# Mixture-of-experts kernel on one core: 39 routed units in each layer instead of 40

## The chip, the core and the metric

The kernel runs on one core of a Trainium2 chip. The metric is the device time of one execution in microseconds. TensorE (PE in the rows) multiplies matrices, VectorE (DVE) and ScalarE (ACT) work elementwise, GpSimd (POOL) and SyncE (SP) mostly issue DMAs here. Every engine runs its own instruction stream in order, and the streams meet only through semaphores that one raises and another waits for.

## The reference

4096 tokens of width 128 pass through four residual blocks: an angular attention, a mixture of experts, a linear attention, and the same mixture of experts again. The mixture is what the change touches, and it is computed twice, once in each "layer":

```
logits = xf @ gate_w + gate_b
top_w, top_i = jax.lax.top_k(logits, K)            # K = 2 of E = 8 experts
gw = jax.nn.softmax(top_w, axis=-1)
combine = (gw[:, :, None] * jax.nn.one_hot(top_i, E)).sum(axis=1)
for e in range(E):
    h = gelu(xf @ w1[e] + b1[e])                   # 128 -> 512
    out = out + combine[:, e:e+1] * (h @ w2[e] + b2[e])   # 512 -> 128
shared = gelu(xf @ ws1 + bs1) @ ws2 + bs2
```

## The kernel before

**Routing by units.** The kernel computes an expert only for the tokens that chose it. GpSimd scatters each token's row twice, once for each chosen expert, into a DRAM buffer `routed_rows` with one region for each expert. A region is then worked on in units of RU = 256 rows. An expert's last unit is usually not full, so the count of units depends on the routing. With 8192 rows in all and at most 255 missing in each of eight regions, no routing needs more than (8192 + 8 * 255) // 256 = 39 units. The count in the code is fixed: `UNITS` rounds 39 up to 40. A table that VectorE makes (`table`, L1669 to L1701) gives each unit its first row (`URI`) and its expert's place in the weights (`UW`) and the biases (`UB`). Units beyond the need are pointed at spare regions behind the eight; their rows are padding whose destinations lie in a spare part of the result buffer. They are computed and stored like any other unit. Which units are needed is known only at run time, but unit 39, the 40th, never is.

**The pads.** `pad_rows` holds PADS = E + SPARE blocks of 256 padding rows, made once by GpSimd. SyncE stores one block at the end of each region in each layer (L467), and one in each of the SPARE = 8 spare regions in layer 0 (L472), before it loads the first unit.

**The routed stage.** `steps` (L61) writes a software pipeline: step s runs each part of the stage for unit s minus that part's lag. With RING = 6 buffers there are some straight steps, then a loop over six steps, then straight steps to the end. For unit u:

- SyncE, `load_rows` (L479 to L490): two DMAs, rows and tail, into ring slot u % 6, once unit u - 6 has left it.
- TensorE, lag 0, `routed_up`: 12 matmuls of 128x256 (L1161 to L1163), into one of three places in PSUM.
- ScalarE, `routed_gelu` (L899): four activations of 128x256.
- VectorE, lag 1, `routed_dest` (L1744) and `routed_split` (L1752, L1755): the hidden values as a high and a low half-precision part.
- TensorE, lag 3, `routed_down`: 24 matmuls of 128x128 (L1177 to L1179); it waits for the split of its unit and for `routed_out` of the unit two before, which frees its PSUM bank.
- VectorE, lag 3, `routed_out` (L1764): scales the result by the gate weight. In a step it comes behind the split of the unit two later.
- GpSimd, `store_results` (L662): two indirect DMAs of 128 rows each, which scatter the results to the tokens' places in `expert_results`.

When the scatters of all units of a layer have landed, SyncE loads `expert_results` back in eight pieces (L499) and VectorE adds them to X (L1432, L1434). In layer 0 the linear attention follows from there, in layer 1 the output.

The functions of both versions, as far as the diff touches them:

Of the kernel before, what the change touches and what calls it, by code (L numbers as in the profile page):

```python
# [16 lines left out]
ALU = mybir.AluOpType  # L17
ACT = mybir.ActivationFunctionType
F32 = mybir.dt.float32
F16 = mybir.dt.float16  # L20
BF16 = mybir.dt.bfloat16
U32 = mybir.dt.uint32
I32 = mybir.dt.int32
# [3 lines left out]
P = 128  # L27
LN_EPS = 1e-5
HEADS, HEAD_DIM = 16, 8
E = 8  # L30
# [4 lines left out]
ROW = 2 * P + 4  # L35
# [6 lines left out]
RS_TILES = 2  # L42
# [5 lines left out]
def wait(engine, semaphore, value):  # L48

    if isinstance(value, int) and value <= 0:  # L50
        return
    engine.wait_ge(semaphore, value)
# [77 lines left out]
def build(nc, x_in, ln_w, ln_b, k_w, q_w, a_bias, w_qkv, w_out, gate_w, gate_b,  # L130
# [5 lines left out]
    assert D == P and S == GT  # L136
    REGION = TOK + RU
    UNITS = (2 * TOK + E * (RU - 1)) // RU
    UNITS = -(-UNITS // 4) * 4
    SPARE = UNITS - 2 * TOK // RU  # L140
    HT = NT // 2
    PADS = E + SPARE
# [10 lines left out]
    with ctx:  # L153
        def sb(name, shape, dt=F32):
            return ctx.enter_context(nc.sbuf_tensor(name, shape, dt))
# [11 lines left out]
        def carve(shape):  # L167

            n = int(np.prod(shape))
            ap = big[:, carved[0]:carved[0] + n]  # L170
            carved[0] += n
            names = "abcd"[:len(shape)]
            sizes = dict(zip(names, shape))
            return ap.rearrange(f"p ({' '.join(names)}) -> p {' '.join(names)}", **sizes)
# [21 lines left out]
        iota_e, region_of = sb("iota_e", [P, 1, E]), sb("region_of", [P, E])  # L196
        down_e = sb("down_e", [P, 1, E])
        chain_on = sb("chain_on", [P, E, NT // 2])
        unit_no = sb("unit_no", [P, UNITS])
        iota_i = sb("iota_i", [P, UNITS], I32)  # L200
        dest = sb("dest", [P, NT, 2], I32)
        halfneg, halfpi, tiny = sb("halfneg", [P, 1]), sb("halfpi", [P, 1]), sb("tiny", [P, 1])
        amax, amaxr = sb("amax", [P, 4]), sb("amaxr", [P, 4])
# [24 lines left out]
        XHL = carve([4 * TPG * ROW]).bitcast(F16).rearrange("p (r t c n) -> p r t c n", r=4, t=TPG, c=2)  # L228
        HF = SC

        pad_rows = carve([PADS * RS_TILES * ROW // 2]).bitcast(F16).rearrange("p (e r n) -> p e r n",
                                                                              e=PADS, r=RS_TILES)
        parts_at = carved[0]
        XNG = carve([2, TPG, D])
        carved[0] = parts_at
# [14 lines left out]
        CN, CNI, NTI = sb("CN", [P, E]), sb("CNI", [P, E], I32), sb("NTI", [P, E], I32)  # L250
        PADF, PADI = sb("PADF", [P, E]), sb("PADI", [P, E], I32)
        NTF, CUM, JUMP = sb("NTF", [P, E]), sb("CUM", [P, E]), sb("JUMP", [P, E])
        UE, UR, UM = sb("UE", [P, UNITS]), sb("UR", [P, UNITS]), sb("UM", [P, E, UNITS])
        URI = sb("URI", [P, UNITS], I32)
        UW, UB = sb("UW", [P, UNITS], I32), sb("UB", [P, UNITS], I32)
        routing_at = carved[0]
        LG, MX = carve([NT, E]), carve([NT, 2])
        OH, CB2, EX, PLACE = carve([2, HT, E]), carve([2, HT, E]), carve([E, HT]), carve([HT, E])
# [6 lines left out]
                                                                                   r=RS_TILES)  # L265
# [79 lines left out]
        def turns(layer, k):  # L345

            return layer * (-(-(UNITS - k) // RING))
# [71 lines left out]
        def table_values(engine_type, table, stride):  # L419

            def values(u, n):
                _, found = nc.values_load_multi_w_load_instructions(
                    table[0:1, bass.ds(u, n)], [engine_type], min_val=0, max_val=(E - 1) * stride,
                    skip_runtime_bounds_check_because="the table's experts are clamped")
                return found
            return values
# [5 lines left out]
        def _(sp):  # L432
# [28 lines left out]
            for layer in range(2):  # L461
# [17 lines left out]
                def load_rows(u, h, k):  # L479

                    wait(sp, s["rh_ready"], layer * UNITS + u - RING + 1)
                    wait(sp, s["dst_ready"], layer * UNITS + u - RING + 1)
                    row = sp.value_load(URI[0:1, bass.ds(u, 1)], min_val=0,
                                        max_val=E * REGION + (SPARE - 1) * RU)
# [29 lines left out]
        def _(pool):  # L514
            made = [0]

            def const(ins):
                made[0] += 1
                ins.then_inc(s["consts_made"], 1)
                pool.wait_ge(s["consts_made"], made[0])  # L520
# [6 lines left out]
                                     base=0, pattern=[[-1, P]], channel_multiplier=1))  # L527
# [5 lines left out]
                                     base=0, pattern=[[1, P]], channel_multiplier=-1))  # L533
# [3 lines left out]
            for view, inner in ((heads, [[0, HEAD_DIM]]), (mask[:, D:D + HEADS], [])):  # L537
                const(pool.affine_select(out=view, in_=view, compare_op=ALU.is_ge, fill=0.0, base=0,
                                         pattern=[[-HEAD_DIM, HEADS]] + inner, channel_multiplier=1))
                const(pool.affine_select(out=view, in_=view, compare_op=ALU.is_ge, fill=0.0,  # L540
                                         base=HEAD_DIM - 1, pattern=[[HEAD_DIM, HEADS]] + inner,
                                         channel_multiplier=-1))
# [3 lines left out]
            const(pool.tensor_scalar(down_e[:, 0, :], iota_e[:, 0, :], -1.0, float(E), ALU.mult, ALU.add))  # L546
            const(pool.memset(chain_on[:], 1.0))
            const(pool.memset(chain_on[:, :, 0:1], 0.0))
            const(pool.iota(iota_i[:], pattern=[[1, UNITS]], base=0, channel_multiplier=0))
            const(pool.tensor_copy(unit_no[:], iota_i[:]))  # L550
            const(pool.iota(dest[:], pattern=[[2 * GT, NG], [2, TPG], [1, 2]], base=0,
                            channel_multiplier=2 * TPG))
# [4 lines left out]
                                     pattern=[[-(E + 1), len(TERMS)]], channel_multiplier=1))  # L557
            const(pool.affine_select(out=term_of[:], in_=term_of[:], compare_op=ALU.is_ge, fill=0.0, base=E,
                                     pattern=[[E + 1, len(TERMS)]], channel_multiplier=-1))
# [34 lines left out]
            def x_scale(n, h, k):  # L594
                if k % 2 == 0:
# [19 lines left out]
                      pattern=[[RU, PADS], [P, RS_TILES], [0, 1]], base=2 * TOK,  # L615
                      channel_multiplier=1).then_inc(s["pads_made"], 1)
# [571 lines left out]
        def _(dve):  # L1188
# [235 lines left out]
            for layer in range(2):  # L1424
# [244 lines left out]
                def table():  # L1669
                    n = [layer * TABLE_STEPS]  # L1670

                    def step(ins):
                        n[0] += 1
                        ins.then_inc(s["table_step"], 1)
                        dve.wait_ge(s["table_step"], n[0])

                    one = slice(0, 1)
                    step(dve.tensor_tensor(CN[one], PADF[one], region_of[one], ALU.subtract))
                    step(dve.tensor_scalar(CNI[one], CN[one], float(RU - 1), None, ALU.add))

                    if layer:
                        dve.wait_ge(s["pads_stored"], 16 * (E * layer + SPARE))
                        for k in range(RING):
                            dve.wait_ge(result_stored[k], 16 * RS_TILES * turns(layer, k))
                    step(dve.tensor_copy(PADI[one], PADF[one]))
                    step(dve.tensor_scalar(NTI[one], CNI[one], RU.bit_length() - 1, None, ALU.logical_shift_right))
                    step(dve.tensor_copy(NTF[one], NTI[one]))
                    step(dve.tensor_tensor_scan(CUM[one], onesf[one, 0:E], NTF[one], 0.0, ALU.mult, ALU.add))
                    step(dve.tensor_scalar(JUMP[one], NTF[one], float(-RU), float(REGION), ALU.mult, ALU.add))
                    begun, by_unit = UM[one], UM[one].rearrange("p e u -> p u e")  # L1690
                    step(dve.tensor_tensor(begun, unit_no[one].unsqueeze(1).to_broadcast([1, E, UNITS]),
                                           CUM[one].unsqueeze(2).to_broadcast([1, E, UNITS]), ALU.is_ge))
                    step(dve.tensor_reduce(UE[one], by_unit, AX.X, ALU.add))
                    step(dve.tensor_tensor(begun, begun, JUMP[one].unsqueeze(2).to_broadcast([1, E, UNITS]),
                                           ALU.mult))
                    step(dve.tensor_reduce(UR[one], by_unit, AX.X, ALU.add))
                    step(dve.scalar_tensor_tensor(UR[one], unit_no[one], float(RU), UR[one], ALU.mult, ALU.add))
                    step(dve.tensor_scalar(UW[one], UE[one], float(E - 1), float(HB * P), ALU.min, ALU.mult))
                    step(dve.tensor_scalar(UB[one], UE[one], float(E - 1), float(HB), ALU.min, ALU.mult))
                    assert n[0] == (layer + 1) * TABLE_STEPS  # L1700
                    dve.tensor_copy(URI[one], UR[one]).then_inc(s["table_ready"], 1)  # L1701

# [12 lines left out]
                def later_table(n, h, k):  # L1715

                    if isinstance(n, int) and n == 7:
                        table()
# [80 lines left out]
```

## Time and profile before

| | us |
|---|---|
| median of three runs | 866.07 |
| lowest, highest | 865.18, 870.05 |
| the profiled execution's own time | 864.79 |
| its span, first to last instruction | 863.0 |

The page of the profile gives TensorE 568.6 us of matmul work (66% of the span), VectorE 579.4 us (67%), ScalarE 403.1 us (47%) and GpSimd 416.4 us (48%). The routed stage of layer 0 lies between about 307 and 465 us of the span, that of layer 1 between about 683 and 842 us. An instruction's row shows its start, its duration, and, in brackets, how long its engine was idle before it and what ended that wait. "Remote" stands for a wait whose end the profile can't put down to an engine.

### The profile page before, as it was taken

Reading aid. Unit: us, or ns where it says so; the run is one execution under the profiler, and the core shown is the slowest. Engines: PE = TensorE matmul, PEld = TensorE weight load, DVE = VectorE, ACT = ScalarE, POOL = GpSimd, SP = SyncE. Lnnn points to the kernel's source line nnn. Section 1 sums busy time; section 2 is a strip of 40 time slices with the busy share of each in tenths; the row PEclk is TensorE's granted clock in tenths of the full one; section 3 lists DMA queues with packets and bytes.
Section 4 is the critical chain, followed back from the end, with each engine's and each line's share of the span. In section 5 each row is a group of like instructions: output and inputs, shape, how many; then the busy total and the mean of one; then the engine's idle time right before and its main releaser. Section 6 shows DMA issues by size and latency. Waiting matters only on the chain.

```text
span 863.0 us, 17109 instructions
## 1 busy us (share of the span) xinstructions
PE 568.6 (66%) x5073; PEld 415.5 (48%) x5074; DVE 579.4 (67%) x1215; ACT 403.1 (47%) x744; POOL 416.4 (48%) x377
## 2 busy tenths in 40 slices
PE   1565726624587788888881678643658998889850
PEld 0222326523354467677671566431235776667740
DVE  5899677977768357676673588856138586676644
ACT  1363899725423155555450577553023374445520
POOL 3097102141788716666664122367734045665670
PEclk9977968965588889999996899766559998999975
DMA  9200000000112523433314100011102233333218
GB/s 290 68 0 0 1 0 1 0 0 10 47 44 78 112 48 79 82 71 74 78 48 150 49 25 2 16 35 50 50 25 74 40 67 66 75 77 69 64 40 295
DMA packets 90829, 51.83 MB, mean 60 GB/s; under 512 B 71482, under 2 KB 79892, under 8 KB 90772
## 3 DMA queue, kind: packets, MB, share of 16 engines
q1 hardware_dynamic: 81556, 32.07, 15.4%
q0 software_dynamic: 9216, 19.02, 7.1%
q8 instruction: 32, 0.52, 0.3%
q14 instruction: 25, 0.20, 0.1%
HBM read 16.28 MB, written 24.30 MB: 47 GB/s over the span
## 4 chain that ended last, share of the span: by engine, by line
PE 38%; DVE 25%; issue 15%; ACT 10%; another core or an unknown queue 5%; DMA 3%; POOL 3%; DVEq 0%; SPq 0%; ACTq 0%; POOLq 0%
PE PC L1177 6%; PE PC L1179 5%; PE PC L1178 4%; PE PA L1161 2%; PE PA L1162 2%; PE PA L1163 2%; DVE PB L1248 2%; PE PA L943 2%; PE PC L1140 2%; DMA RR<-expert_results 2%; ACT SC L734 2%; DVE big L1657 1%; ACT RR L730 1%; POOL routed_rows L626 1%
## 5 line engine op out<-in xcount | busy, mean ns | idle before, releaser
L662 POOL DMA_INDIRECT expert_results<-RR,DG x160 | 186.7, 1167 | 153.9 <-DVE RR L1764 112.3
L626 POOL DMA_INDIRECT routed_rows<-big,SLQ x128 | 142.3, 1112 | 83.0 <-DVE SLQ L1619 45.8
L899 ACT ACTIVATE SC<-PA,B1T,scl 128x256 f32<-128x256 f32 x216 | 104.1, 568 | 103.5 <-remote 60.3
L1177 PE MATMUL PC<-W2H,big 128*128 x640 | 125.4, 224 | 15.9 <-issue 10.7
L1178 PE MATMUL PC<-W2H,big 128*128 x640 | 123.5, 222 | 7.8 <-issue 7.6
L1179 PE MATMUL PC<-W2L,big 128*128 x640 | 123.3, 221 | 8.2 <-issue 7.9
L1755 DVE SCALAR_TENSOR_TENSOR big<-SC,scl,big 128x1024 f16<-128x1024 f32 x80 | 102.8, 1285 | 2.8
L784 ACT ACTIVATE SC<-PA,B1T,scl 128x512 f32<-128x512 f32 x64 | 45.1, 775 | 112.2 <-remote 62.5
L1764 DVE SCALAR_TENSOR_TENSOR RR<-PC,scl,DG 128x256 f32<-128x256 f32 x80 | 38.3, 481 | 79.1 <-remote 66.7
L1177 PEld LDWEIGHTS PC<-W2H,big 128*128 128x128 f16 x640 | 62.9, 98 | 36.5 <-issue 27.9
L1140 PE MATMUL PC<-W2H,big 128*128 128x128 f16 x256 | 54.6, 241 | 26.7 <-DVE big L1657 18.8
L1179 PEld LDWEIGHTS PC<-W2L,big 128*128 128x128 f16 x640 | 62.9, 98 | 14.2 <-issue 13.0
L1178 PEld LDWEIGHTS PC<-W2H,big 128*128 128x128 f16 x640 | 63.6, 99 | 11.8 <-issue 11.3
L1752 DVE TENSOR_SCALAR big<-SC,scl 128x1024 f16<-128x1024 f32 x80 | 60.8, 759 | 9.7 <-ACT SC L899 9.5
L899 ACT ACTIVATE SC<-PB,B1T,scl 128x256 f32<-128x256 f32 x104 | 50.4, 568 | 31.9 <-remote 20.0
L1161 PE MATMUL PA<-big,W1H 128*128 128x256 f16 x216 | 59.6, 276 | 4.1 <-issue 3.8
L1142 PE MATMUL PC<-W2H,big 128*128 128x128 f16 x256 | 54.7, 242 | 9.3 <-issue 9.3
L1162 PE MATMUL PA<-big,W1H 128*128 128x256 f16 x216 | 59.4, 275 | 0.7 <-issue 0.5
L1163 PE MATMUL PA<-big,W1L 128*128 128x256 f16 x216 | 59.5, 275 | 0.4 <-issue 0.2
L1141 PE MATMUL PC<-W2L,big 128*128 128x128 f16 x256 | 54.6, 241 | 7.7 <-issue 7.6
L963 PE MATMUL PC<-QW,PB 128*128 128x128 f32 x256 | 37.1, 314 | 33.1 <-DVE PB L1402 17.5
L963 PEld LDWEIGHTS PC<-QW,PB 128*128 128x128 f32 x256 | 35.7, 227 | 35.2 <-DVE PB L1402 18.3
(262 smaller groups left out, 1383.6 us busy)
## 6 DMA issues: line engine op xcount, KB each, us to landing
RR<-expert_results SPq DMA_DIRECT2D x16, 512.0 KB, 4.6
routed_rows<-big SPq DMA_DIRECT2D x24, 130.0 KB
expert_results<-RR,DG POOLq DMA_INDIRECT x160
X<-n_L_attn_a_hidden_states SPq DMA_DIRECT2D x2, 1024.0 KB, 6.8
big<-in_L_ffn_w SPq DMA_DIRECT2D x1, 2048.0 KB, 8.5
routed_rows<-big,SLQ POOLq DMA_INDIRECT x128
out_x<-X SPq DMA_DIRECT2D x8, 256.0 KB, 4.8
big<-routed_rows SPq DMA_TRANSPOSE x80
```

The lines of the kernel that those rows point to most:

```text
L626: pool.indirect_dma_start(routed, bass.IndirectOffsetOnAxis(ap=SLQ[:, slot, t, c:c + 1], axis=0), XHL[:, slot, t, c, :].bitcast(I32), None ...
L662: pool.indirect_dma_start(results, bass.IndirectOffsetOnAxis(ap=DG[:, k, r, 0:1], axis=0), YT[:, k, r, :], None).then_inc(result_stored[k] ...
L899: ins = act.activation(HF[:, k % 3, b * RU:(b + 1) * RU], up_out(k, b), ACT.Gelu, scale=INV1, bias=B1T[:, bass.ds(b1_at + b, 1)])
L963: last = pe.matmul(PC[slot][:, t * D:(t + 1) * D], PB[:, slot, b, t * P:(t + 1) * P], QW[:, b, :], start=(b == 0), stop=(b == HB - 1))
L1140: pe.matmul(o, hh, W2H[:, c:c + P], start=(b == 0), stop=False)
L1161: pe.matmul(o, W1H[:, at], xh, start=True, stop=False)
L1162: pe.matmul(o, W1H[:, at], xl, start=False, stop=False)
L1163: last = pe.matmul(o, W1L[:, at], xh, start=False, stop=True)
L1177: pe.matmul(o, hh, W2H[:, at], start=(b == 0), stop=False)
L1178: pe.matmul(o, hl, W2H[:, at], start=False, stop=False)
L1179: last = pe.matmul(o, hh, W2L[:, at], start=False, stop=(b == HB - 1))
L1755: dve.scalar_tensor_tensor(HL3[:, k % 3, :], HF[:, k % 3, 0:HB * RU], SH, HH3[:, k % 3, :], ALU.mult, ALU.subtract).then_inc(s["rhl_ready" ...
```

## The change

`UNITS` becomes 39, without the rounding to a multiple of four. The tables that hold a value for each unit keep 40 entries under a new name, `TABLE`, so the VectorE instructions that make them are the same. What follows from `UNITS` changes with it: SPARE is 7 instead of 8, PADS 15 instead of 16, `pad_rows` keeps the room of 16 blocks and is filled and stored for 15, and both DRAM buffers are 256 rows shorter. The places of all other tiles in SBUF stay.

```
-    UNITS = -(-UNITS // 4) * 4
+    TABLE = -(-UNITS // 4) * 4
...
-        unit_no = sb("unit_no", [P, UNITS])
-        iota_i = sb("iota_i", [P, UNITS], I32)
+        unit_no = sb("unit_no", [P, TABLE])
+        iota_i = sb("iota_i", [P, TABLE], I32)
...
-        pad_rows = carve([PADS * RS_TILES * ROW // 2]).bitcast(F16).rearrange("p (e r n) -> p e r n",
-                                                                              e=PADS, r=RS_TILES)
+        pad_rows = carve([(PADS + PADS % 2) * RS_TILES * ROW // 2]).bitcast(F16).rearrange(
+            "p (e r n) -> p e r n", r=RS_TILES, n=ROW)[:, 0:PADS, :, :]
...
-        UE, UR, UM = sb("UE", [P, UNITS]), sb("UR", [P, UNITS]), sb("UM", [P, E, UNITS])
+        UE, UR, UM = sb("UE", [P, TABLE]), sb("UR", [P, TABLE]), sb("UM", [P, E, TABLE])
```

The remaining lines of the diff write `TABLE` for `UNITS` in the same way.

VectorE's stream where layer 0's routed stage ends and the combine (L1432) begins; rows with a minus are of the kernel before, those without a sign are in both:

```order
 L1752 TENSOR_SCALAR big<-SC,scl 128x1024
 L1755 SCALAR_TENSOR_TENSOR big<-SC,scl,big 128x1024
-L1764 SCALAR_TENSOR_TENSOR RR<-PC,scl,DG 128x256
-L1744 COPY DG<-big 128x4
-L1752 TENSOR_SCALAR big<-SC,scl 128x1024
-L1755 SCALAR_TENSOR_TENSOR big<-SC,scl,big 128x1024
 L1764 SCALAR_TENSOR_TENSOR RR<-PC,scl,DG 128x256 x3
 L1432 TENSOR_TENSOR X<-RR,X 128x512
```

One step of the pipeline is gone, so the last three outputs follow directly on the split of unit 38.

GpSimd's stream at the same place, the end of its loop over six units and what follows it (12288 and 12032 are the rows of the result buffer):

```order
 L84 REGISTER_ALU
 L84 COMPARE_AND_BRANCH
-L662 DMA expert_results<-RR,DG 12288x128 x8
+L662 DMA expert_results<-RR,DG 12032x128 x6
 L633 MEMSET big 128x8
 L567 TENSOR_TENSOR RS<-VA,halfneg 128x4 x13
```

Two scatters fewer stand between the loop and layer 1's first instruction. The loops themselves have as many turns as before on every engine; layer 1 ends in the same way.

## Rows read from the trace of the kernel before

**Rows 1.** The page: the span, and in 40 slices TensorE's granted clock in tenths

```profile
span 863.0 us, 17109 instructions
...
PEclk9977968965588889999996899766559998999975
```

**Rows 2.** The page's group of GpSimd's result scatters: busy, mean ns, idle before

```profile
L662 POOL DMA_INDIRECT expert_results<-RR,DG x160 | 186.7, 1167 | 153.9 <-DVE RR L1764 112.3
```

**Rows 3.** Timeline of VectorE, layer 0, outputs of two units that lie three apart

```profile
414.26 0.48 DVE L1764 SCALAR_TENSOR_TENSOR RR<-PC,scl,DG 128x256 f32<-128x256 f32 x1 [2.96 <-remote]
...
425.25 0.48 DVE L1764 SCALAR_TENSOR_TENSOR RR<-PC,scl,DG 128x256 f32<-128x256 f32 x1 [3.18 <-remote]
```

**Rows 4.** Timeline of GpSimd, the end of layer 0's routed stage

```profile
450.85 0.96 POOL L662 DMA_INDIRECT expert_results<-RR,DG  x1 [1.17 <-issue]
452.11 1.24 POOL L662 DMA_INDIRECT expert_results<-RR,DG  x1 [0.30 <-issue]
453.66 1.73 POOL L662 DMA_INDIRECT expert_results<-RR,DG  x1 [0.30 <-issue]
455.70 0.96 POOL L662 DMA_INDIRECT expert_results<-RR,DG  x1 [0.30 <-DVE RR L1764]
...
463.29 0.96 POOL L662 DMA_INDIRECT expert_results<-RR,DG  x1 [0.31 <-issue]
```

**Rows 5.** Timeline of VectorE, the end of layer 0's routed stage

```profile
449.57 0.48 DVE L1764 SCALAR_TENSOR_TENSOR RR<-PC,scl,DG 128x256 f32<-128x256 f32 x1 [2.00 <-remote]
...
450.83 1.28 DVE L1755 SCALAR_TENSOR_TENSOR big<-SC,scl,big 128x1024 f16<-128x1024 f32 x1
...
452.49 0.75 DVE L1752 TENSOR_SCALAR big<-SC,scl 128x1024 f16<-128x1024 f32 x1
453.27 1.28 DVE L1755 SCALAR_TENSOR_TENSOR big<-SC,scl,big 128x1024 f16<-128x1024 f32 x1
454.55 0.88 DVE L1764 SCALAR_TENSOR_TENSOR RR<-PC,scl,DG 128x256 f32<-128x256 f32 x2
457.79 0.48 DVE L1764 SCALAR_TENSOR_TENSOR RR<-PC,scl,DG 128x256 f32<-128x256 f32 x1 [2.36 <-PE PC L1179]
```

**Rows 6.** Timeline of the SyncE queue: layer 0's results are loaded back

```profile
465.76 9.75 SPq L499 DMA_DIRECT2D RR<-expert_results  x6
```

**Rows 7.** Timeline of GpSimd, the end of layer 1's routed stage

```profile
828.84 1.73 POOL L662 DMA_INDIRECT expert_results<-RR,DG  x1 [0.30 <-issue]
830.87 0.96 POOL L662 DMA_INDIRECT expert_results<-RR,DG  x1 [0.30 <-issue]
...
836.56 0.96 POOL L662 DMA_INDIRECT expert_results<-RR,DG  x1 [2.19 <-DVE RR L1764]
...
840.36 0.96 POOL L662 DMA_INDIRECT expert_results<-RR,DG  x1 [0.30 <-issue]
```

**Rows 8.** Timeline of VectorE, the end of layer 1's routed stage

```profile
830.88 0.48 DVE L1764 SCALAR_TENSOR_TENSOR RR<-PC,scl,DG 128x256 f32<-128x256 f32 x1 [1.14 <-remote]
835.29 0.88 DVE L1764 SCALAR_TENSOR_TENSOR RR<-PC,scl,DG 128x256 f32<-128x256 f32 x2 [3.93 <-PE PC L1179]
```

**Rows 9.** Timeline of TensorE, first and last of unit 39's 12 up matmuls

```profile
822.30 0.27 PE L1161 MATMUL PA<-big,W1H 128*128 128x256 f16 x1
...
823.50 0.27 PE L1163 MATMUL PA<-big,W1L 128*128 128x256 f16 x1
```

**Rows 10.** Windows: us, busy and (count) of PE, PEld, DVE, ACT, POOL; clock; DMA

```profile
716.00:720.00 4.00, 2.61 (x12) 1.49 (x13) 1.35 (x3) 1.02 (x3) 1.45 (x2) 0.51 0.30 66
832.00:834.00 2.00, 2.00 (x21) 1.72 (x19) 0.00 (x0) 0.00 (x0) 1.54 (x2) 0.52 0.20 66
```

**Rows 11.** Timeline of SyncE's queue and GpSimd, before layer 0's first unit

```profile
282.03 5.40 SPq L472 DMA_DIRECT2D routed_rows<-big  x8
...
303.53 1.35 POOL L626 DMA_INDIRECT routed_rows<-big,SLQ  x1 [0.30 <-issue]
...
306.97 1.31 SPq L486 DMA_TRANSPOSE big<-routed_rows  x1
```

More of the change, by code:

```diff
@@ L252, in build @@
         NTF, CUM, JUMP = sb("NTF", [P, E]), sb("CUM", [P, E]), sb("JUMP", [P, E])
-        UE, UR, UM = sb("UE", [P, UNITS]), sb("UR", [P, UNITS]), sb("UM", [P, E, UNITS])
-        URI = sb("URI", [P, UNITS], I32)
-        UW, UB = sb("UW", [P, UNITS], I32), sb("UB", [P, UNITS], I32)
+        UE, UR, UM = sb("UE", [P, TABLE]), sb("UR", [P, TABLE]), sb("UM", [P, E, TABLE])
+        URI = sb("URI", [P, TABLE], I32)
+        UW, UB = sb("UW", [P, TABLE], I32), sb("UB", [P, TABLE], I32)
         routing_at = carved[0]
@@ L548, in _ @@
             const(pool.memset(chain_on[:, :, 0:1], 0.0))
-            const(pool.iota(iota_i[:], pattern=[[1, UNITS]], base=0, channel_multiplier=0))
+            const(pool.iota(iota_i[:], pattern=[[1, TABLE]], base=0, channel_multiplier=0))
             const(pool.tensor_copy(unit_no[:], iota_i[:]))
@@ L1690, in table @@
                     begun, by_unit = UM[one], UM[one].rearrange("p e u -> p u e")
-                    step(dve.tensor_tensor(begun, unit_no[one].unsqueeze(1).to_broadcast([1, E, UNITS]),
-                                           CUM[one].unsqueeze(2).to_broadcast([1, E, UNITS]), ALU.is_ge))
+                    step(dve.tensor_tensor(begun, unit_no[one].unsqueeze(1).to_broadcast([1, E, TABLE]),
+                                           CUM[one].unsqueeze(2).to_broadcast([1, E, TABLE]), ALU.is_ge))
                     step(dve.tensor_reduce(UE[one], by_unit, AX.X, ALU.add))
-                    step(dve.tensor_tensor(begun, begun, JUMP[one].unsqueeze(2).to_broadcast([1, E, UNITS]),
+                    step(dve.tensor_tensor(begun, begun, JUMP[one].unsqueeze(2).to_broadcast([1, E, TABLE]),
                                            ALU.mult))
```

## The prediction

> **What bounds the kernel now.** I began with the page: its clock line says that TensorE is throttled in places, and no engine is busy all the time [rows 1]. So the change is worth what its unit costs in its own stage. GpSimd's group of result scatters comes next: 160 of them, 1167 ns each, and 112.3 us in which GpSimd waited for VectorE's output [rows 2]. Inside the stage GpSimd is therefore fed by the others and doesn't bound.
>
> The timeline of VectorE gives the pace: outputs three units apart start at 414.26 and 425.25 us, 10.99 us for three, or 3.66 us a unit [rows 3]. Both rows show a wait of about 3 us put down to "remote". The stage runs two units quickly and then all wait. What they wait for the profile doesn't name; TensorE's rows show its gaps as "issue", so I take it for something in TensorE's supply of instructions. It is not needed for the sum, but it is the largest unknown in it.
>
> At the end of a layer the pace is another. In layer 0 GpSimd's last gap is the 1.17 us before 450.85. From there nine more scatters follow each other with 0.30 us between them, to 463.29 + 0.96 = 464.25 us, while VectorE's last output is done at 458.27 [rows 4, 5]. The reader is to see that the last scatter starts 5 us after its data is there: over the last units GpSimd is the bound. SyncE's load of the results starts at 465.76, 1.5 us after the last scatter, and everything after it hangs on it [rows 6]. So layer 0 ends by GpSimd's queue, and this is where a unit less is to be priced.
>
> In layer 1 GpSimd is behind for a while too, but catches up: its scatter at 836.56 waited 2.19 us for VectorE [rows 7], whose outputs of units 38 and 39 come together at 835.29, after 3.93 us of waiting for TensorE [rows 8]. So there the end is TensorE's, then GpSimd's four last scatters.
>
> **The change, part by part.**
>
> Layer 0. It removes two scatters, 1.26 us each from start to start (455.70 to 463.29 is six steps), 2.53 us [rows 4]. It also removes VectorE's split of unit 39, 452.49 to 454.55 [rows 5]. Two scatters lie beside that split and take 1.24 and 1.73 us; the seven from 455.70 on have no split beside them and take 0.96 us each [rows 4]. So without it I let both take 0.96: 0.28 + 0.77 = 1.05 us. A scatter beside the split before it, at 450.85, takes 0.96 all the same, so the bound from below for this term is nothing. I take the full 1.05, since all the slow ones in this end have a split of unit 39 beside them.
>
> The Trainium skill, "GPSIMD Engine Reference", section Specifications, says that GpSimd shares its SBUF interfaces with VectorE and that the two contend when a VectorE instruction uses two ports or reads two SBUF inputs. The second half of the split reads two, and the 1.73 us beside it agrees, while the 0.96 us at 450.85 does not. By the rule the end of layer 0 gains 3.6 us, with scatters that don't care for VectorE it gains 2.5.
>
> Is the data there in time? The first start stays at 450.85, since TensorE's and VectorE's streams up to the output of unit 35 at 449.57 are the same. GpSimd then runs eight scatters, to 450.85 + 7 * 1.265 + 0.96 = 460.67 us. The last pair would start at 458.4; the output of unit 38 is in the pair at 454.55 today and can't be later with less ahead of it [rows 5]. So the layer ends 464.25 - 460.67 = 3.6 us earlier. Bounds: 2.5 and the pace of a unit, 3.66.
>
> Layer 1. The same two scatters go, 2.53 us, if the output of unit 38 still comes at 835.29. It won't: TensorE no longer runs unit 39's up products, 822.30 to 823.77, 1.47 us ahead of the last downs [rows 9], nor VectorE the split. I take 1.47 us earlier for unit 38's output: it ends at 834.30 in place of 835.77, its scatters start 0.79 us later (836.56 now) at 835.09, and the last ends at 837.32, against 840.36 + 0.96 = 841.32 now [rows 7, 8]. That is 4.0 us. The bound from above is GpSimd without any wait: from 828.84, unit 36's first scatter, six scatters to 836.13, 5.2 us. The bound from below is 2.5. The truth is nearer the middle, because 835.29 is late for a reason of its own: TensorE ran unit 39's down at a clock of 0.52, the lower of its two levels, 1.2 GHz [rows 10], and the output of unit 38 came only then. With no unit 39 that stretch may vanish.
>
> At nothing: ScalarE's four activations (it waits through most of the stage), SyncE's loads of unit 39, six ring slots ahead, and the table, whose instructions are the same. The pads: eight spare blocks are issued from 282.03 to 287.43 us, and the first unit's load at 306.97 comes after GpSimd's last row scatter at 303.53 [rows 11]. One block less leaves some 16 us of slack as it is; without that cover it would be 5.40 / 8 = 0.7 us. The smaller fill of `pad_rows` is under the same cover.
>
> Between the two ends everything moves earlier as a whole. Sum: 3.6 + 4.0 = 7.6 us. Against the profiled execution, 864.79 us with 1.8 us outside its span, this gives 857.2. The median of the runs is 1.3 us above that execution, so I predict 858.5.
>
> **The rivals.**
>
> A, the forecast: the ends shorten by their scatters and a bit, 2.5 to 5.2 us a layer. In all 5.1 to 8.8 us, so 857.3 to 861.0. Chance 0.55.
>
> B, more than that: the last unit also takes one of the common waits or a clock drop with it. A wait is worth about 3 us [rows 3]. A drop: between 716 and 720 us at a clock of 0.51 TensorE began 12 matmuls, where 36 in 3.66 us would be 39, which is 4 * 27 / 39 = 2.8 us lost [rows 10]. One or both on top of A's middle give 10 to 13 us, 853 to 856. Layer 1's own drop at 832 speaks for it. Chance 0.17.
>
> C, the waits fall elsewhere. Layer 1's instructions stand 36 matmuls and their loads earlier in TensorE's stream, and its work starts 3.6 us earlier. If the common waits depend on the place in the stream, they move, and layer 1 may catch one or two drops more, at 2.8 us each: 7.6 less 2.8 or 5.6 is a gain of 2 to 4.8 us, 861.3 to 864.1. For it speaks that layer 1 shows drops in its stage and layer 0 none [rows 1], with the same instructions: their timing is delicate. Chance 0.18.
>
> The Trainium skill, "Runtime: NRT & Kernel Launch", section Instruction fetch mechanics, says that instructions stream in by fixed blocks and that a taken branch outside the blocks at hand stalls the engine. That is C's mechanism, or B's. No row here shows a fetch as the cause, so it has no price beside C's.
>
> D, no gain at all: the start of the combine hangs on something other than the last scatter. The 1.5 us from scatter to load speaks against it [rows 4, 6]. 866, chance 0.06.
>
> E, slower: C's mechanism alone, far enough. It decides from the point at which new drops cost 7.6 + 4.3 = 11.9 us, five at 2.8 us, in the two loops: 870.5 or more. The whole stage of layer 1 has few such places today. Chance 0.04.
>
> **How the numbers follow.** What a measurement of this kernel tells from no change is about 0.5%, 4.3 us: 861.7 and 870.4 are the marks. Faster: A, B and half of C, 0.81. Slower: E, 0.04. The same: the rest, 0.15. The range 854 to 862.5 holds A, most of B and nearly half of C, 0.8 in all.
>
> **What would show it.** In the profile after: 156 result scatters; layer 0's eight scatters from about 450.9 us on without a gap, all near 0.96 us, the last ending near 460.7, and the load of the results 1.5 us behind; layer 1's stage of 39 units at the pace of 3.66 us, its last scatter ending some 7.6 us earlier than 841.3. If the two scatters in layer 0 stay slow, the term of 1.05 is wrong; if unit 38's output in layer 1 still waits long for TensorE, the 4.0 is. The sum fails altogether if layer 1's stage takes another time per unit than before, for then the waits and the clock decide and not the ends.

## The result and the profile after

The change takes 858.91 us, median of 20 runs (851.06 to 879.51), against 866.15 us (860.75 to 878.38) for the kernel before. The ratio is 0.9881 with a 95% interval of 0.9852 to 0.991. The medians lie 7.2 us apart, and I had forecast 7.6 us and 858.5 us. Both kernels scatter by 2 to 3% from run to run, and the ratio compares their undisturbed runs alone, which is why it gives somewhat more (10 us) than the medians.

The page of the profile after, with the rows that answer to [rows 1] and [rows 2]:

```profile
span 854.8 us, 16860 instructions
...
PEclk9987968965579579999998699786559999999985
...
L662 POOL DMA_INDIRECT expert_results<-RR,DG x156 | 182.2, 1168 | 152.9 <-DVE RR L1764 113.2
```

There are 156 result scatters in place of 160, of the same mean duration. The clock line has its low places at the same stages but for one: the 14th slice, from about 280 us on, reads 8 before and 5 after. The end of layer 0's routed stage, which answers to [rows 4], on GpSimd:

```profile
452.68 0.96 POOL L662 DMA_INDIRECT expert_results<-RR,DG  x1 [2.36 <-DVE RR L1764]
453.95 1.34 POOL L662 DMA_INDIRECT expert_results<-RR,DG  x1 [0.30 <-issue]
455.60 1.73 POOL L662 DMA_INDIRECT expert_results<-RR,DG  x1 [0.30 <-issue]
457.63 0.96 POOL L662 DMA_INDIRECT expert_results<-RR,DG  x1 [0.30 <-DVE RR L1764]
...
465.22 0.96 POOL L662 DMA_INDIRECT expert_results<-RR,DG  x1 [0.30 <-issue]
```

and on VectorE, for [rows 5]:

```profile
454.43 0.74 DVE L1752 TENSOR_SCALAR big<-SC,scl 128x1024 f16<-128x1024 f32 x1
455.21 1.28 DVE L1755 SCALAR_TENSOR_TENSOR big<-SC,scl,big 128x1024 f16<-128x1024 f32 x1
456.45 0.88 DVE L1764 SCALAR_TENSOR_TENSOR RR<-PC,scl,DG 128x256 f32<-128x256 f32 x2
459.73 0.48 DVE L1764 SCALAR_TENSOR_TENSOR RR<-PC,scl,DG 128x256 f32<-128x256 f32 x1 [2.41 <-PE PC L1179]
```

The reader is to see a picture that is the same as before and not a shorter one: a first scatter after a wait, then nine that follow with 0.30 us between them, the second and third of them slow and beside a split. Only the unit numbers are lower by one, because this queue now begins with unit 34.

Layer 1 ends in the same way, which it did not before [rows 7]:

```profile
819.86 0.96 POOL L662 DMA_INDIRECT expert_results<-RR,DG  x1 [1.91 <-DVE RR L1764]
821.13 1.24 POOL L662 DMA_INDIRECT expert_results<-RR,DG  x1 [0.30 <-issue]
822.67 1.73 POOL L662 DMA_INDIRECT expert_results<-RR,DG  x1 [0.30 <-issue]
824.71 0.96 POOL L662 DMA_INDIRECT expert_results<-RR,DG  x1 [0.30 <-DVE RR L1764]
...
832.30 0.96 POOL L662 DMA_INDIRECT expert_results<-RR,DG  x1 [0.30 <-issue]
```

The windows of the same end, for [rows 10] (us, then busy and count of PE, PEld, DVE, ACT and POOL, then TensorE's granted clock), show it at the higher level, or nearly, until TensorE's last down:

```profile
820.00:824.00 4.00, 3.00 (x44) 2.41 (x42) 3.96 (x7) 0.75 (x2) 3.39 (x3) 1.00 0.10 33
824.00:828.00 4.00, 1.75 (x24) 1.42 (x24) 0.91 (x3) 0.00 (x0) 3.09 (x4) 0.97 0.15 49
```

The table sets the stretches of the two profiled executions side by side, each from a row's start or end, in us:

| stretch | before | after | difference |
|---|---|---|---|
| to layer 0's first output | 323.79 | 328.84 | +5.1 |
| from there to the end of its last scatter | 140.46 | 137.34 | -3.1 |
| to layer 1's first output | 232.37 | 230.44 | -1.9 |
| from there to the end of its last scatter | 144.70 | 136.64 | -8.1 |
| to the end of the span | 21.68 | 21.54 | -0.1 |

The sum, -8.2 us, is near the forecast, but two of the five differences lie where the change does little or nothing, and layer 1 gave twice what I had worked out. Part of this goes with TensorE's clock. Between 280 and 300 us, ahead of layer 0's first output, the granted clock is 0.87 and 0.81 in the two halves before and 0.58 and 0.59 after. In layer 1's stage TensorE stood at the lower level for about 14 us before, in three places, and for about 4 us after, in one:

```profile
712.00:724.00 12.00, 8.79 (x72) 6.59 (x71) 6.32 (x12) 3.87 (x8) 5.88 (x6) 0.72 0.36 73
774.00:782.00 8.00, 6.00 (x53) 4.68 (x50) 4.69 (x8) 3.76 (x8) 4.46 (x5) 0.79 0.37 88
832.00:836.00 4.00, 2.23 (x21) 1.72 (x19) 0.71 (x2) 0.00 (x0) 1.92 (x2) 0.51 0.15 49
```

```profile
764.00:770.00 6.00, 4.91 (x44) 4.10 (x45) 4.83 (x8) 2.70 (x6) 2.65 (x4) 0.72 0.24 48
```

(the first three before, the last after). Layer 0's stage had no such place before and two of about 3 us each after, so its -3.1 us isn't clean either. Whether the change moves these places or chance does, one pair of executions can't tell. That is what the experiments are for.

### The profile page after: what moved, and what is told of

It is laid out like the page before. It is cut to its first block, busy times and chain, and to the rows that moved or that the text cites. A ratio compares the mean times of both kernels' runs of the same rounds, so it can differ in the third digit from the quotient of the medians.

```text
span 854.8 us, 16860 instructions
## 1 busy us (share of the span) xinstructions
PE 558.6 (65%) x5001; PEld 408.7 (48%) x5002; DVE 573.2 (67%) x1207; ACT 399.6 (47%) x736; POOL 408.9 (48%) x373
## 4 chain that ended last, share of the span: by engine, by line
PE 38%; DVE 27%; issue 17%; ACT 8%; POOL 4%; DMA 3%; another core or an unknown queue 3%; ACTq 0%; DVEq 0%; POOLq 0%; SPq 0%
PE PC L1177 5%; PE PC L1179 4%; PE PC L1178 4%; PE PA L1161 3%; PE PA L1163 2%; PE PA L1162 2%; DVE BN L1197 2%; PE PC L1140 2%; DVE PB L1248 2%; PE PA L943 2%; PE PC L1142 2%; ACT SC L734 2%; DMA RR<-expert_results 2%; PE PC L1141 1%
## 5 line engine op out<-in xcount | busy, mean ns | idle before, releaser
L662 POOL DMA_INDIRECT expert_results<-RR,DG x156 | 182.2, 1168 | 152.9 <-DVE RR L1764 113.2
L899 ACT ACTIVATE SC<-PA,B1T,scl 128x256 f32<-128x256 f32 x208 | 100.4, 567 | 99.7 <-remote 56.7
L1177 PE MATMUL PC<-W2H,big 128*128 x624 | 120.0, 222 | 14.0 <-issue 9.3
L1178 PE MATMUL PC<-W2H,big 128*128 x624 | 118.2, 220 | 9.0 <-issue 8.9
L1179 PE MATMUL PC<-W2L,big 128*128 x624 | 117.7, 220 | 7.6 <-issue 7.5
L1755 DVE SCALAR_TENSOR_TENSOR big<-SC,scl,big 128x1024 f16<-128x1024 f32 x78 | 100.2, 1285 | 2.8
L1177 PEld LDWEIGHTS PC<-W2H,big 128*128 128x128 f16 x624 | 61.0, 98 | 36.5 <-issue 28.4
L1140 PE MATMUL PC<-W2H,big 128*128 128x128 f16 x256 | 52.5, 236 | 24.1 <-DVE big L1657 18.1
L1178 PEld LDWEIGHTS PC<-W2H,big 128*128 128x128 f16 x624 | 61.5, 99 | 11.6 <-issue 11.1
L1179 PEld LDWEIGHTS PC<-W2L,big 128*128 128x128 f16 x624 | 61.0, 98 | 9.7 <-issue 9.0
L1142 PE MATMUL PC<-W2H,big 128*128 128x128 f16 x256 | 52.1, 234 | 13.7 <-issue 13.7
L1161 PE MATMUL PA<-big,W1H 128*128 128x256 f16 x208 | 58.0, 279 | 2.5 <-issue 2.2
L1162 PE MATMUL PA<-big,W1H 128*128 128x256 f16 x208 | 57.9, 278 | 0.0
L1141 PE MATMUL PC<-W2L,big 128*128 128x128 f16 x256 | 52.0, 234 | 8.1 <-issue 8.1
```

Of the source, the lines that this page charges most:

```text
L662: pool.indirect_dma_start(results, bass.IndirectOffsetOnAxis(ap=DG[:, k, r, 0:1], axis=0), YT[:, k, r, :], None).then_inc(result_stored[k] ...
L899: ins = act.activation(HF[:, k % 3, b * RU:(b + 1) * RU], up_out(k, b), ACT.Gelu, scale=INV1, bias=B1T[:, bass.ds(b1_at + b, 1)])
L1140: pe.matmul(o, hh, W2H[:, c:c + P], start=(b == 0), stop=False)
L1161: pe.matmul(o, W1H[:, at], xh, start=True, stop=False)
L1162: pe.matmul(o, W1H[:, at], xl, start=False, stop=False)
L1177: pe.matmul(o, hh, W2H[:, at], start=(b == 0), stop=False)
```

## The experiments

All ratios are to the kernel before on the same chip. Which chip the first measurement ran on, called the first here, is not known. The first eight kernels ran on one chip, called the second here, on which the kernel before takes 794 to 795 us, the ninth (fewer matmuls) on one with 892 us, and the last three on one with 793 us. The second chip is 71 us faster than the first measurement, and the runs scatter by 1% there.

**One layer at a time.** The count of units is made a value for each layer; the pads and the table stay as before.

```
-                steps(pe, UNITS, RING, [(0, routed_up), (3, routed_down)],
+                steps(pe, UN[layer], RING, [(0, routed_up), (3, routed_down)],
...
+    UN = (39, 40)          # and (40, 39) in the second kernel
```

> 39 units in layer 0 alone, 40 in layer 1, pads as before. Theory 1 (the ends: each layer gets shorter by what GpSimd's last scatters and the step ahead of them cost) expects 3.6 us less than before, a ratio of 0.996, and a routed stage of layer 0, from its first output to the end of its last scatter, of 136.9 us against 140.46, with layer 1's stage as before. Rival (the change moves the waits in TensorE's supply, and the gain lies where those fall) expects nothing fixed for layer 0: its stage within 1 us of 140.5, and a difference in layer 1 though nothing is taken out there.

> 39 units in layer 1 alone, 40 in layer 0, pads as before. Theory 1 expects 4.0 us less than before, a ratio of 0.995, layer 0's stage at 140.5 us and layer 1's at 140.7 against 144.70. Rival (layer 1 lost a clock drop or two by luck or by the moved code, which is why its stage took 136.6 us in the profile after) expects layer 1's stage anywhere from 136 to 146 us, its length set by how many stretches at the lower clock it has.

Measured: 792.4 us for layer 0 alone, ratio 0.9973 (0.9957 to 0.9989), 2.6 us by the medians; 792.07 us for layer 1 alone, 0.9969 (0.9952 to 0.9986), 3.0 us. Each layer gives about the same, each less than I had forecast for it. Layer 1's stage, first output to the end of the last scatter, took 123.9 us in the first of these profiles with all its 40 units and 118.2 us in the second with 39. The profile of the kernel before on this chip (below) has 120.5 us. So a profiled stage of the same 40 units varies by 3 us, and the 8.1 us of the table above are not a unit's. On this chip the variation lies in the first outputs of layer 1: the second comes 4.1 us after the first in the profile with 123.9 us and 2.5 us after it in the one with 120.5 us, while the 27 units from the seventh output on take 82.7 us in both. Layer 0's stage varies less and shows the unit. With 40 units it took 121.3 and 122.6 us in two profiles of this chip, with 39 units 117.5, 118.2 and 118.7 us in three.

**The pads and the buffers.** The change with `SPARE = TABLE - 2 * TOK // RU`, which keeps 16 pad blocks and the longer buffers.

> 39 units in both layers but 16 pad blocks, 8 of them spare, and both DRAM buffers as long as before. If the pads are hidden, as I argued, this is as fast as the change: a ratio of 0.988 to before. Rival (the pads or the buffers' length cost or give something: in the profile after, layer 0's first output comes at 328.84 us against 323.79) expects the first output near 323.8 here, and a ratio of 0.983.

Measured: 788.79 us, 0.993 (0.9906 to 0.9953). The first output comes at 321.39 us. The unaltered change gave 0.9927 on the same chip (below), with its first output at 320.91. The smaller pads are worth nothing that can be measured, and the 5.1 us by which layer 0 began later in the profile after didn't come again. It goes with the lower clock ahead of it.

**The scatters alone, and everything but the scatters.** The first kernel computes all 40 units and leaves out the two scatters of unit 39. The second loads and computes 39 units, and GpSimd still issues 40 pairs; the last pair sends an earlier unit's results to spare rows.

```
-                steps(pool, UNITS, RING, [(0, store_results)])
+                steps(pool, 39, RING, [(0, store_results)])     # first kernel; 40 in the second
...
+    UN = (39, 39)                                                # second kernel
...
-                            results, bass.IndirectOffsetOnAxis(ap=DG[:, k, r, 0:1], axis=0),
+                            results, bass.IndirectOffsetOnAxis(
+                                ap=nowhere[:, r:r + 1] if extra else DG[:, k, r, 0:1], axis=0),
```

> All 40 units computed in both layers, but GpSimd leaves out the two scatters of unit 39 (the unit is padding, its results are used nowhere; SyncE waits for its output before it loads the results back). Theory 1 expects 2.5 us less a layer, 5.1 in all, a ratio of 0.994: most of the gain is in GpSimd's queue. Rival (the pace is TensorE's up to the end, and the scatters only trail it) expects no gain in layer 1 and at most 1 us in layer 0: 0.999 or more.

> 39 units are loaded and computed in each layer, but GpSimd still does 40 units' scatters: the last pair sends ring slot 3, which holds an earlier unit's results, to spare rows that nothing reads. It takes out all of unit 39 but its scatters. Theory 1 expects the rest of the gain, what leaving out the scatters alone did not give (4.75 us of 6.2): 1 to 2 us, a ratio of 0.998. Rival (TensorE's and VectorE's step is what is won, the scatters follow) expects nearly the whole gain, 0.993 to 0.994.

Measured: 790.28 us without the scatters, 0.9942 (0.9921 to 0.9962), 4.7 us less; 793.3 us with them but without the unit, 0.9989 (0.9968 to 1.0009), 0.7 us less, which is no difference that can be told from none. Together they make 5.4 us, about what the change gives here (5.6, below). Both rivals are out, the one that expected 0.999 of the first kernel and the one that expected 0.993 to 0.994 of the second. Most of the gain is in GpSimd's queue at the ends, as the forecast had it. The end of layer 0 in the trace of the second kernel, VectorE's last output and GpSimd's last scatters:

```profile
432.78 0.48 DVE L1774 SCALAR_TENSOR_TENSOR RR<-PC,scl,DG 128x256 f32<-128x256 f32 x1 [1.43 <-PE PC L1189]
```

```profile
438.86 0.96 POOL L672 DMA_INDIRECT expert_results<-RR,DG  x1 [0.30 <-issue]
440.12 0.96 POOL L672 DMA_INDIRECT expert_results<-RR,nowhere  x1 [0.31 <-issue]
441.38 0.96 POOL L672 DMA_INDIRECT expert_results<-RR,nowhere  x1 [0.30 <-issue]
```

The last output is done at 433.26 us, and GpSimd needs 9 us more for what has piled up. That TensorE and VectorE finished a unit earlier is worth next to nothing while the 80 scatters stay.

**The change again, and the kernel before for its trace.**

> The change itself, unaltered, on this chip. On the chip of the last runs (kernel before at 795 us there) 39 units in layer 0 alone gave 2.6 us, in layer 1 alone 3.0 us, and both with 16 pad blocks 6.2 us. Theory 1 (each layer's end) expects the two to add up, 5.6 to 6.2 us less, a ratio near 0.993, on a chip of that kind, and about 0.988 where the kernel before takes 866 us. Rival (the smaller pads and buffers matter) expects it to differ from the kernel with 16 pad blocks by over 1 us.

> The kernel before, unaltered: a ratio of 1.000, and its trace on the same chip. If the chip is like that of the last runs, it has none of the waits put down to remote in the routed stages, a stage of layer 0 near 121 us where the first chip took 140.5, and the pace of a unit near 3.0 us in place of 3.66. If the waits belong to the program and not to the chip, they are there again.

Measured: the change 788.42 us, 0.9927 (0.9906 to 0.9949); the kernel before 794.04 us, 0.9993 (0.997 to 1.0017). The two layers alone add up to 5.6 us, and this is 5.6 us. (The profile of the change doesn't show it in layer 1: its stage took 121.3 us with 39 units there, against 120.5 us with 40. Again it is the first outputs, 5.4 us apart against 2.5, and the 27 units behind the seventh take 82.6 and 82.7 us. Layer 1's 3.0 us rest on the medians alone.) The trace of the kernel before on this chip has none of the waits put down to remote in its routed stages. Its groups by line between 330 and 438 us of layer 0 (busy, mean ns, idle before) show what is missing:

```profile
L662 POOL DMA_INDIRECT expert_results<-RR,DG x72 | 69.9, 971 | 39.2 <-DVE RR L1764 22.3 <-issue 17.0
L1177 PE MATMUL PC<-W2H,big 128*128 x289 | 54.8, 222 | 3.0 <-issue 2.4 <-DVE RR L1764 0.3
L1178 PE MATMUL PC<-W2H,big 128*128 x289 | 54.1, 219 | 0.0
L1179 PE MATMUL PC<-W2L,big 128*128 x289 | 53.9, 219 | 0.0
```

The same groups in the kernel before of the first measurement, between 330 and 460 us:

```profile
L662 POOL DMA_INDIRECT expert_results<-RR,DG x74 | 87.7, 1185 | 43.1 <-DVE RR L1764 24.3 <-issue 18.8
L1177 PE MATMUL PC<-W2H,big 128*128 x291 | 55.7, 221 | 7.9 <-issue 5.2 <-DVE RR L1764 1.0 <-DVE big L1755 0.7
L1179 PE MATMUL PC<-W2L,big 128*128 x292 | 54.9, 219 | 4.0 <-issue 4.0
L1178 PE MATMUL PC<-W2H,big 128*128 x291 | 54.8, 219 | 4.7 <-issue 4.6
```

The matmuls take the same time, at the full clock in both. On the first chip TensorE stands still inside its down products, where nothing of the program is waited for (L1178 and L1179 are the middle of a run of 24); here it never does. One such place on the first chip, ahead of the wait of [rows 3]; the starts are 0.6 to 0.75 us apart where the next ones are 0.06 us apart:

```profile
411.70 0.22 PE L1177 MATMUL PC<-W2H,big 128*128 x1 [0.44 <-issue]
412.41 0.22 PE L1178 MATMUL PC<-W2H,big 128*128 x1 [0.49 <-issue]
412.47 0.22 PE L1179 MATMUL PC<-W2L,big 128*128 x1
413.22 0.22 PE L1177 MATMUL PC<-W2H,big 128*128 x1 [0.54 <-issue]
...
413.39 0.22 PE L1177 MATMUL PC<-W2H,big 128*128 x1
414.00 0.22 PE L1178 MATMUL PC<-W2H,big 128*128 x1 [0.39 <-issue]
```

The pace of a unit follows: three outputs of layer 0 on this chip, 3.0 us apart:

```profile
424.63 0.48 DVE L1764 SCALAR_TENSOR_TENSOR RR<-PC,scl,DG 128x256 f32<-128x256 f32 x1 [0.42 <-PE PC L1179]
...
427.66 0.48 DVE L1764 SCALAR_TENSOR_TENSOR RR<-PC,scl,DG 128x256 f32<-128x256 f32 x1 [0.39 <-PE PC L1179]
...
430.67 0.48 DVE L1764 SCALAR_TENSOR_TENSOR RR<-PC,scl,DG 128x256 f32<-128x256 f32 x1 [0.47 <-PE PC L1179]
```

against 3.66 us in [rows 3]. And the end of its layer 0, and that of the change on this chip, both on GpSimd:

```profile
431.94 0.96 POOL L662 DMA_INDIRECT expert_results<-RR,DG  x1 [0.79 <-DVE RR L1764]
433.20 0.95 POOL L662 DMA_INDIRECT expert_results<-RR,DG  x1 [0.30 <-issue]
...
440.78 0.95 POOL L662 DMA_INDIRECT expert_results<-RR,DG  x1 [0.30 <-issue]
```

```profile
429.78 0.96 POOL L662 DMA_INDIRECT expert_results<-RR,DG  x1 [0.81 <-DVE RR L1764]
431.04 0.95 POOL L662 DMA_INDIRECT expert_results<-RR,DG  x1 [0.30 <-issue]
...
438.61 0.95 POOL L662 DMA_INDIRECT expert_results<-RR,DG  x1 [0.30 <-issue]
```

Eight scatters follow each other in both. The queue of the end has the same length and the same durations; it begins 111.50 us after the first output (320.44) before and 108.87 us after it (320.91) with the change.

**Seven units fewer.** For this input's routing 36 units in layer 0 and 37 in layer 1 are enough. `UN = (36, 37)` computes only those; it is right for this routing and not for every one.

> Only as many units as this input's routing needs, 36 in layer 0 and 37 in layer 1, seven fewer than before; pads as before. The theory of the ends says that the first unit taken out is worth GpSimd's two scatters and a bit, and each further one the pace of the stage: at 3.0 us a unit seven are worth 20 us, a ratio of 0.975; at 3.66, 26 us, 0.970. Rival (only what stands in GpSimd's queue at the end is won, 2.5 us a unit) expects 17.5 us, 0.978.

Measured: 774.05 us, 0.9737 (0.9711 to 0.9763), 19.9 us less by the medians, 2.85 us a unit. The interval (20.9 us for the ratio itself, 18.8 to 22.9) holds 20 us and leaves out 17.5, the 2.5 us a unit of the rival. It also holds seven units at the full 3.05 us that a unit takes in the middle of the stage, 21.3 us. The change's two units gave 2.8 us each, and the five beyond them (788.42 to 774.05 us) 2.9 us each. So the first unit taken out is worth as much as the later ones, near the pace of the stage.

**Fewer matmuls.** The routed stage without the product with the low part of w1, so the hidden values lose that part.

```
-                        pe.matmul(o, W1H[:, at], xl, start=False, stop=False)
-                        last = pe.matmul(o, W1L[:, at], xh, start=False, stop=True)
+                        last = pe.matmul(o, W1H[:, at], xl, start=False, stop=True)
```

> 40 units as before, but TensorE leaves out one of three up products in the routed stage (the low part of the weights, 4 of a unit's 36 matmuls, 0.44 us of a unit by the spacing of 0.11 us), so the hidden values lose the low part of w1. On this chip a unit takes 3.0 us, GpSimd's pair of scatters 2.53 us, and TensorE's 36 matmuls about 3.0. The theory that TensorE sets the pace of the stage and GpSimd only its end expects 0.4 us less a unit, 30 to 34 us in all, a ratio near 0.96. Rival (GpSimd sets the pace too, since in some layers its scatters follow each other nearly all the time) expects under 5 us less, 0.994 or more.

Measured: 885.39 us, 0.9947 (0.9911 to 0.9982), on yet another chip, on which the kernel before takes 891.87 us. The 0.4 us a unit is not won there: 6.5 us in all are 0.08 us a unit. The number is the rival's (0.994 or more) and not the theory's 0.96. But the expectation had the other chip's pace in mind, so this run doesn't decide between TensorE and GpSimd. VectorE's timeline has the waits of the first chip again, here in two outputs three units apart:

```profile
381.94 0.48 DVE L1763 SCALAR_TENSOR_TENSOR RR<-PC,scl,DG 128x256 f32<-128x256 f32 x1 [2.83 <-remote]
...
392.60 0.48 DVE L1763 SCALAR_TENSOR_TENSOR RR<-PC,scl,DG 128x256 f32<-128x256 f32 x1 [2.86 <-remote]
```

10.66 us for three units, near the 10.99 us of [rows 3], though each unit has 32 matmuls in place of 36 and three units 1.3 us less of matmul time. That most of the matmul time taken out goes into these waits fits, but it isn't shown: there is no trace of the kernel before on this chip. TensorE also stood at the lower clock level for some 17 us of layer 0's stage and 24 us of layer 1's in this profile, and that may have cost as much.

**A busier TensorE stream, and once more the pair.**

```
+                        settle(pe, s["pe_passed"])     # twice before each of a unit's four up blocks
+                        settle(pe, s["pe_passed"])
```

> 40 units as before, with 8 instructions more in a unit on TensorE (semaphore increments that nobody waits for), on top of some 92. If the gaps of 0.7 us come with the supply of instructions, a fixed number of instructions in a period of about 10.7 us, a unit gets longer by about 8 of 92 on a chip that has the gaps: 0.3 us a unit, 20 to 25 us in all, a ratio near 1.025. Where the chip has no gaps TensorE only issues them: under 5 us more. Rival (the gaps come with the matmuls, or with time) expects under 5 us more on either kind of chip.

> The kernel before, unaltered, for its trace beside the next two. Two kinds of chip have been seen: one at 795 us, a unit at 3.0 us and no gaps of 0.7 us between TensorE's matmuls, and two at 866 and 892 us, a unit at 3.6 us, with such gaps about every 100 matmuls. This run shows which kind this one is.

> The change, unaltered. The theory that a unit is worth the pace of the chip's stage expects 6 us less (ratio 0.993) where a unit takes 3.0 us, and 7.3 us less (0.992) where it takes 3.66; the first measurement, 0.988 with an interval of 0.985 to 0.991, would then have had 2 to 3 us of drift in it. Rival (the gaps and clock drops add a gain of their own on chips that have them) expects 0.988 again on such a chip.

Measured, on the chip of 793 us, which has no gaps either: the kernel before 794.05 us, 1.0009 (0.9991 to 1.0027); the change 790.66 us, 0.995 (0.9928 to 0.9972); the extra instructions 879.66 us, 1.1086 (1.1061 to 1.1111). The last misses what both theories gave by far, and what it was made for, the supply of instructions on a chip with gaps, it can't tell here. Its TensorE timeline says why it is slow:

```profile
401.18 0.28 PE L1163 MATMUL PB<-big,W1H 128*128 128x256 f16 x1
401.30 0.27 PE L1164 MATMUL PB<-big,W1H 128*128 128x256 f16 x1
401.41 0.27 PE L1165 MATMUL PB<-big,W1L 128*128 128x256 f16 x1
401.75 0.28 PE L1163 MATMUL PB<-big,W1H 128*128 128x256 f16 x1
```

From one up block to the next it is 0.57 us where three matmuls at 0.11 us take 0.33, so a pair of increments takes 0.24 us, 0.12 each, and a unit's eight about 1.0 us. In the middle of the stage the 27 units from the seventh output on take 114.1 us against 82.0, 1.2 us more for each unit. The whole run gives 86.5 us over 640 increments, 0.135 us each, but some of it is TensorE waiting for the split and for ScalarE, 6.5 us in those 27 units, which in the kernel before it hardly does.

That does answer the question left by the run before: on a chip without the gaps, 1.0 us more in TensorE's stream makes a unit at least as much longer, so TensorE had nothing to spare. The kernel before on this chip shows the same without any edit. Here are its windows in the middle of layer 0's and of layer 1's stage (TensorE's busy time first, GpSimd's fifth):

```profile
340.00:420.00 80.00, 76.74 (x949) 65.84 (x947) 67.47 (x106) 50.55 (x105) 51.19 (x53) 1.00 0.42 89
666.00:746.00 80.00, 76.73 (x943) 65.42 (x942) 67.38 (x107) 50.25 (x104) 63.97 (x52) 1.00 0.43 89
```

TensorE is busy for 96% of both. GpSimd's scatters take longer in layer 1 (1222 ns on average between 660 and 755 us, against 973 ns between 330 and 430 us) and follow each other there with hardly a wait, yet a unit takes 3.05 us in layer 1 and 3.04 in layer 0. So on such a chip TensorE sets the pace of the stage and GpSimd does not.

The change itself gives less here than two units at that pace, 6.1 us or 0.9923, would be: 4.0 us by the ratio, whose interval ends at 0.9928, and 2.5 us by the medians. Why this chip gives less than the second, with the same pace, is open.

## Why the prediction held, step by step

**The bound at the ends.** Right. GpSimd's queue outlasts VectorE's last output by 6 us in layer 0, and without each layer's last two scatters alone 4.7 of 5.6 us are won on the second chip. What the prediction did not say is why the queue piles up there: once the last unit's up products are through, the downs of the last units come one upon another (two outputs from 454.55 on, the last at 457.79 [rows 5]), while each pair of scatters still takes 2.53 us.

**Two scatters a layer, 2.53 us.** Right in size: 4.7 us by measurement for the four (3.0 to 6.3 by the interval), 5.1 forecast.

**Unit 39's split, 1.05 us.** This is the step that failed, and with it the sentence that the first start of the queue stays at 450.85. I took the two slow scatters of [rows 4] to vanish with the split beside them. In the profile after they stand there again, 1.34 and 1.73 us, beside the split of unit 38, and the queue begins with unit 34 and not with unit 35. The end keeps its form whichever unit is the last. What took the term's place is that the whole end moves by a unit of the stage's pace. From layer 0's first output to the start of the queue it was 127.06 us (450.85 less 323.79), and after 123.84 us (452.68 less 328.84): 3.2 us, and the queue behind it is as long as before, 13.4 and 13.5 us. The stage after holds two places at the lower clock, so the 3.2 us alone prove little. The second chip, with no such place, has the same picture, with 2.6 us and queues of 9.8 us. The sum for the layer, 3.6 us, was near by luck: the pair and the wrong 1.05 happen to add up to nearly the pace, 3.66.

**Layer 1, 4.0 us.** This step failed too. The mechanism, 1.47 us of up products ahead of the last down, was argued from an end that was disturbed, with a drop of the clock in it. Without that drop layer 1 ends as layer 0 does, on GpSimd's queue: in the profile after, and in the kernel before on the second chip, where both layers' last scatters end 5.4 us after VectorE's last output. On the second chip layer 1 gives 3.0 us and layer 0 2.6. The profile's 8.1 us for layer 1 holds one unit of 3.66 us and some 4.5 us more: the 27 units from the seventh output on took 99.6 us before and 95.1 us after. That goes with the 14 us at the lower clock before and the 4 us after. Whether the change or chance moved them isn't settled. That the sum of 7.6 us lies near the medians' 7.2 is in part luck, then: the two layers' terms are both wrong in their working, and the ratio says 10 us.

**At nothing: the pads.** Right. The kernel with 16 pad blocks is as fast as the change.

**The rivals.** A was right in kind. Where it could be measured finely it is at or below A's lower end of 5.1 us: 5.6 us of 794 on the second chip, 4.0 of 793 on the last. B, a common wait or a drop won on top, may be in the first measurement, whose ratio of 0.9881 is below the 0.9927 and 0.995 of the two faster chips; a unit there costs 3.66 and not 3.0 us, which gives 7.3 us or 0.9915, just outside its interval. The lower clock of layer 1's stage before speaks for it, but that the change brings it has not been shown. C and E, waits that move and eat the gain, did not show in any of three measurements of the change, unless the small gain on the last chip is theirs. D fell.

**The common waits.** I took the 3 us waits for something in TensorE's supply of instructions and left them open. They are not the program's: the same kernel has them on two chips and not on two others. They come in the middle of runs of matmuls that wait for nothing. That the supply of instructions is the cause was not shown. The run meant for it fell on a chip without gaps.

## What to carry to other kernels

In a software pipeline like this one a unit less is worth about the pace of the stage, whichever engine's queue ends it, and the fill and drain around it stay as they are. Price it from the distance of two equal events in the middle of the stage, not from what the last unit's instructions take or what they slow down. And let a fixed count of padded units be no larger than the worst case needs: the rounding to four cost a unit in each layer, 0.5 to 1.2% here.

## What the runs showed of the hardware

- One program, one input: 866, 794, 892 and 793 us in four measurements, the last three known to be on different chips. On the two slower ones TensorE stops within runs of matmuls for about 0.7 us at a time, several times in a row, mostly 70 to 110 matmuls apart, and VectorE and ScalarE wait about 3 us for it. The Trainium skill, "Runtime: NRT & Kernel Launch", section Instruction fetch mechanics, has an engine stream its instructions in fixed blocks, mostly hidden; gaps that come back after a similar count of instructions might fit that, but no run here shows it, nor why two chips are free of them.
- An increment of a semaphore as an instruction of its own between matmuls takes TensorE 0.12 us by the rows (0.135 us by the whole run), more than the 0.11 us from one matmul of 256 columns to the next. VectorE, ScalarE and GpSimd use the same form once a unit in this kernel, TensorE not.
- A scatter of GpSimd beside VectorE's split takes 0.96 us or up to 1.73 us. On the second chip, in layer 0, scatters that start with the split take 0.96 us throughout (mean 971 ns for 72). The split alone does not make one slow; when in it the scatter starts seems to, which was not tried. In layer 1 on the chip of 793 us they take 1.22 us on average, and a unit takes no longer for it.
